# Two attentions and three mixtures of experts on one core: the turn of the probabilities, the value product and the turn of the result move by one block of products each in TensorE's order

## What is computed

```python
n1 = _layernorm(x, ln1_w, ln1_b)
rw = _gating(n1.reshape(b * t, c), smha_sim, smha_gates, MIN_ATT).reshape(b, t, -1)
q = jnp.einsum('btc,ech,bte->bth', n1, q_proj, rw)
k = jnp.einsum('btc,ech,bte->bth', n1, k_proj, rw)
v = jnp.einsum('btc,ech,bte->bth', n1, v_proj, rw)
scores = jnp.einsum('bth,bsh->bts', q, k) * scale
scores = jnp.where(causal, scores, -jnp.inf)
attn = jnp.einsum('bts,bsh->bth', jax.nn.softmax(scores, axis=-1), v)
attn_out = jnp.einsum('bth,ehc,bte->btc', attn, o_proj, rw)
hs = x + attn_out
```

## Time and profile before

| | |
|---|---|
| time, median of 3 runs | 3059.33 us (3059.03 to 3063.7) |
| span of the profiled execution | 3021.6 us |
| that execution's own time | not listed apart; the median lies 37.7 us over the span |
| PE busy | 2857.8 us (95%) |
| PE weight loads busy | 2563.3 us (85%) |
| VectorE busy | 2286.3 us (76%) |
| ScalarE busy | 1877.8 us (62%) |
| GpSimd busy | 1564.7 us (52%) |

### The profile page before, as it was taken

The page is one execution under the profiler, slowest core; times in us unless marked ns, Lnnn a source line. Parts: engine busy times, 40 slices in busy tenths (PEclk is TensorE's granted clock), DMA queues, the critical chain, the costliest instruction groups (busy, mean ns, idle before and its releaser), DMA issues. The chain is left out here.

```text
span 3021.6 us, 85335 instructions
## 1 busy us (share of the span) xinstructions
PE 2857.8 (95%) x26943; PEld 2563.3 (85%) x26944; DVE 2286.3 (76%) x6211; ACT 1877.8 (62%) x6970; POOL 1564.7 (52%) x1816
## 2 busy tenths in 40 slices
PE   6999999889999999997999999999989999998778
PEld 5878888689999999996999999999988888886556
DVE  6988888877777777776777777777768888888745
ACT  5888888755555555555344444444458888887735
POOL 3565656466666666665322222222226666654556
PEclk9999999999999999998999999999999999999779
DMA  6000000010000000000000000000010000000245
GB/s 222 16 19 15 17 14 14 2 62 11 10 10 10 10 11 12 10 10 25 25 11 10 10 10 10 10 10 10 5 47 18 17 14 14 17 14 2 93 140 150
DMA packets 56235, 86.43 MB, mean 29 GB/s; under 512 B 6944, under 2 KB 42785, under 8 KB 55458
## 3 DMA queue, kind: packets, MB, share of 16 engines
q1 hardware_dynamic: 49284, 66.47, 7.0%
q0 software_dynamic: 6528, 16.92, 1.5%
q10 hardware_dynamic: 288, 1.31, 0.1%
HBM read 57.25 MB, written 28.48 MB: 28 GB/s over the span
## 5 line engine op out<-in xcount | busy, mean ns | idle before, releaser
L562 ACT ACTIVATE L_probs<-bank,L_neg_max 128x128 f32<-128x128 f32 x2048 | 716.8, 403 | 150.4 <-DVE L_neg_max L636 149.9
L562 ACT ACTIVATION_READ_ACCUMULATOR L_probs<-bank,L_neg_max 128x1 f32 x2048 | 497.8, 243 | 0.0
L642 DVE COPY L_probsT<-bank 128x512 f32<-128x512 f32 x512 | 353.0, 689 | 136.6 <-PE bank L460 81.5
L1719 ACT ACTIVATE M_inter<-bank 128x512 f32<-128x512 f32 x256 | 153.3, 599 | 438.8 <-PE bank L69 387.9
L67 PE MATMUL bank<-W_hi,M_nT_hi 128*128 128x384 f32 (+1 forms) x1024 | 370.2, 362 | 8.3 <-DVE M_qkv L1345 4.4
L636 DVE TENSOR_REDUCE L_neg_max<-bank 128x4 f32<-128x512 f32 x512 | 327.6, 682 | 30.7 <-PE bank L437 30.6
L69 PE MATMUL bank<-W_lo,M_nT_hi 128*128 128x384 f32 (+1 forms) x1024 | 346.8, 339 | 0.0
L68 PE MATMUL bank<-W_hi,M_nT_lo 128*128 128x384 f32 (+1 forms) x1024 | 346.6, 338 | 0.0
L447 PE MATMUL bank<-constants,L_probs 128*128 128x128 f32 x2048 | 327.3, 284 | 12.9 <-ACT L_probs L562 10.1
L1778 DVE TENSOR_TENSOR M_inter_lo<-M_inter,M_inter_hi 128x512 fp32r<-128x512 f32 x256 | 207.1, 809 | 168.5 <-ACT M_inter_hi L1720 158.2
L67 PE MATMUL bank<-W_hi,M_inter_hi 128*128 128x256 f32 x1024 | 290.5, 284 | 11.8 <-DVE M_inter_lo L1778 11.0
(11 more groups left out here) (334 smaller groups left out, 9144.7 us busy)
## 6 DMA issues: line engine op xcount, KB each, us to landing
L_ctx_in<-in_ctx SPq DMA_DIRECT2D x64, 256.0 KB, 2.6
M_tile<-M_sorted SPq DMA_DIRECT2D x72, 130.0 KB, 2.3
x_all<-in_x SPq DMA_DIRECT2D x8, 1024.0 KB, 10.5
raw_weights<-in_weights SPq DMA_DIRECT2D x2, 4096.0 KB, 15.6
hs<-M_hs SPq DMA_DIRECT2D x64, 128.0 KB, 1.7
M_hs<-hs SPq DMA_DIRECT2D x32, 256.0 KB, 2.6
M_sorted<-M_fill SPq DMA_DIRECT2D x16, 130.0 KB, 2.1
raw_weights<-in_weights SPq DMA_DIRECT2D x1, 2048.0 KB, 8.0
```

Of the source, the lines that this page charges most:

```text
L562: last = act.activation(probs[:, k % UNITS, i, :], score_bank[u][:, i, :], ACT.Exp, bias=neg_max[:, u, i:i + 1], scale=-1.0, accum_out=sum ...
L642: dve.tensor_copy(probsT[:, k % 2], pT_ps[k % UNITS]).then_inc(pT_ready, 1)
L1719: act.activation(inter[:, e % 2], up_bank[e % 2], ACT.Gelu).then_inc(M.inter_ready, 1)
```

## The change

Three conditions in PE's `step` change their number. Nothing is added or removed, and the orders of the four other engines are the same.

```diff
                         if e == 2:
                             score(s)
-                        if e == 4:
+                        if e == 5:
                             turn_p(s)
-                        if e == 5:
+                        if e == 6:
                             times_v(s, b)
-                        if e == 6:
+                        if e == 7:
                             turn_a(s)
```

## The result

| | before | after |
|---|---|---|
| median | 3059.61 us (3059.03 to 3063.7, 4 runs) | 3080.71 us (3078.9 to 3082.63, 4 runs) |
| profiled execution | span 3021.6 us | 3078.9 us, span 3076.9 us |
| ratio | | 1.0066, 95% interval 1.0053 to 1.008 |

What follows compares the result with a forecast made beforehand. PE was taken to bound the mixture attention. Losses of 6.4 us at P4, 12.6 at O1 and 0.6 outside the loop gave 19.6 us on 3059.3, so 3079 us, range 3064 to 3090.

Steps and rivals of the forecast that it cites:

- Part 1: Turn of the probabilities, moved behind P4, no longer fills P4's wait for VectorE: 0.11 us in 58 steps, 6.4 us.
- Part 2, the chain: From the later value product through `normalize` to `rest_a`: `normalize` waits and starts 0.82 us later, `rest_a` ends at 710.81.
- Part 3, O1's stall: O1's load waits for `rest_a`: 0.36 us in even steps, including 0.18 for a register-operation wait, 0.09 in odd; 12.6 us.
- The sum: Whole kernel: 6.4 us at P4, 12.6 at O1, 0.6 in steps outside the loop; 19.6 us slower.
- The median lies 37.7 us over the span, which the change does not touch: Whole kernel: the median 3059.33 exceeds the profile's span 3021.6 by 37.7 us, taken as unaffected.
- The rule on weight loads pulled ahead: PE's queue: if loads passed waits, stalled blocks would start about 0.1 us sooner, sum about 14 us; judged contradicted.
- What stays covered: P0's load behind `weigh_even(6)`: still no stall, with a cover of 0.1 to 0.2 us.
- O1 covered: Rival at O1: no stall there, only the loss at P4 remains, 3065.7 us; chance 0.2.
- The delay spreads: Rival: ScalarE's later rounding delays q and k copies past the scores, 0.3 us more a step, 3096 us; chance 0.12.
- Faster: Rival at P4: the 0.12 us stall belongs to the turn, so moving it saves 7 us, 3052.4; chance 0.04.
- Nothing measurable: Rival: VectorE's chain from the scores runs 0.1 us shorter, no wait grows, O1 covered; chance 0.05.
- What bounds the stage: Mixture attention: PE bounds it, busy 100.00 of 100 us, with one short stall at P4, 0.12 us in the mean.

Runs made afterwards that it cites:

- e2: Kernel before with the turn of the probabilities behind P4 and the value product three matmuls later, behind O3: 3029.86 us beside 3022.98, ratio 1.002.
- e3: Kernel after with `rest_a` put ahead of the statistics and the guard on VectorE: 3031.07 us beside 3022.98 for the kernel before, ratio 1.0025.
- e6: Kernel after with PE's wait for `rest_a` placed behind the bank's wait, on the matmul: 3042.66 us beside 3023.65 for the kernel before, ratio 1.0062.
- e5: Kernel before with O3 put between the turn of the probabilities and P4 on PE: 3018.45 us beside 3022.98, ratio 0.999.
- e7: Kernel after with O3 ahead of P4 and `rest_a` ahead of statistics and guard: 3022.99 us beside 3023.65 for the kernel before, ratio 0.9991.
- e8: Kernel before with O3 ahead of P4 and the normalised input's turn ahead of the result's turn: 3022.28 us beside 3023.65, ratio 0.9995.
- e11: Kernel before with only the two sums of `weigh_out(0)` put ahead of the gates on VectorE: 3127.82 us beside 3063.48, ratio 1.021.

## Why the prediction was right, step by step

- **What bounds the stage** (PE, read by starts and not by busy share): right. The busy share after is 99.87 of 100 at clock 1.00 with 2.9% lost.
- **Part 1, 0.11 us a step, 6.4 us:** right. P4's load stays 0.05 behind `weigh_even(2)`, and e2 alone costs 6.9 us and 0.11 of period.
- **Part 2, the chain:** `normalize` waits for the value product, and starts 0.42 us behind it (1040.49 to 1040.91), as said. From there to `rest_a` 2.01 us in even and 1.91 in odd steps were needed where 1.97 and 1.88 had been taken over. e3 shows that this queue is the cause.
- **Part 3, O1's stall, 0.36 and 0.09 us:** the mis-sized term. Measured 0.28 and 0.17. The step that failed is "I take that 0.18 for PE's even steps too", the price of a wait on a register operation. The load starts 0.13 us behind `rest_a` in even and 0.12 in odd steps, not 0.23 and 0.05; the form of the wait makes 0.01, and e6 confirms it. Even: 0.10 too much there, 0.04 too little in the chain; odd: 0.07 and 0.03 too little. The periods show the same: forecast 0.47 longer in even and 0.20 in odd steps, measured 0.40 and 0.32. By chance the halves cancel: 28 x 0.28 + 28 x 0.17 = 12.6 us, just the forecast sum. That part of the hit is luck. VectorE's row, the nearest at hand, was no guide for PE's queue.
- **The sum:** 6.4 + 12.6 + 0.6 = 19.6 for 21.1 measured; by the period 58 x 0.36 = 20.9. Of the 0.36 some 0.02 a step are in neither part; by the starts 0.01 of them stand at P4 and 0.01 where the turn of the result now stands directly ahead of the turns of the input. Why is not shown.
- **"The median lies 37.7 us over the span, which the change does not touch":** wrong as a reading. Around the span are only 2 us; the rest is, as far as the profiles show, another chip's last stage. It did no harm, since the sum was set on the median.
- **The rule on weight loads pulled ahead:** the load did not pass the wait. At P4 and at O1, each listed as a wait 53 times, the load starts 0.05 and 0.11 to 0.13 us behind the row that releases it.
- **What stays covered:** P0 did not stall after the change, and `weigh_even(6)` followed `rest_a` at once (1043.12 behind 1042.92 + 0.28, overlapping). P0's load starts 0.16 to 0.19 us behind its end, for 0.05 where it waits, so the cover left was 0.11 to 0.14, within the 0.1 to 0.2 forecast. The slim cover was real: it is the bound that e5, e7 and e8 ran into.
- **Rivals.** O1 covered: fell, its line has 53 entries. The delay spreads: fell, no wait at the scores or copies. Faster: fell; with the turn gone from ahead of P4 the load still sat behind VectorE. But the number that this rival gave for moving work ahead of P4, 7 us, was too high as well: e5's period gives 1.2. Nothing measurable: fell, with both waits grown and 21.1 us measured.

## What to carry to other kernels

Moving small work later in a full engine's order costs what it was hiding: look for the wait that it fills (here 0.11 us at P4), and for what hangs on it at the far end of another engine's queue (here `rest_a`, behind statistics that nobody needed). Read a saturated engine by the distance of starts, or by the count of instructions in a fixed stretch, never by its busy share. And when one stall is taken away, expect the next one close behind: of 0.12 us a step only 0.02 to 0.03 came back, until the chain on a third engine was cut too.

## What the runs showed of the hardware that I had not expected

- Some small VectorE operations that start beside a two-input sum of GpSimd end only with that sum: 0.53 us for 0.23 (L934, two inputs), 0.72 for 0.17 (L937, two inputs), 0.93 (L950). A maximum with one input beside the same sum keeps its 0.17, and weighings that read a bank and one operand keep their 0.62. The kernel before pays for this as well: L954, eight columns, takes 0.65 us beside a sum there in all 54 steps, and 0.17 in e11, where no sum runs. What GpSimd's sums collide with is therefore part of any edit that moves them; in e11 it was about half of 2.1%.
- Two signals of VectorE reach PE's weight loads at different distances from the rows' ends, 0.05 us for `weigh_even(2)` and 0.11 to 0.13 for `rest_a`. The place of the wait is not the reason; the reason stays open.
- The same kernel has a median of 3063.5 us on one chip and of 3023.0 to 3025.5 on three others. In the profiles the last stage is what differs: 222.4 to 231.4 us in those with spans of 3016 to 3042 us, 263.4 to 265.3 in those at 3077 us and more, with 1372 to 1376 us for the stages ahead of it in all. Why is not shown. Sums made on one profile's span have to be set on the median of the same chip.
